# Two layers of conditioned attention on one core: the row maxima handed out to the steps by a length model, and two of the norms computed by GpSimd alone

## The chip, the cores and the metric

The kernel runs on 1 core of one Trainium2 chip. The metric is the device time of one execution in microseconds (us).

## The reference

x is (2, 1024, 256): two batches of 1024 tokens with 256 channels, all float32. Two layers follow each other, and both end in the same kind of tail.

```python
# layer 0: softmax attention with 16 heads of 16 channels
xn = layer_norm(x, norm_w, norm_b)
q, k = xn @ q_w + q_b, xn @ k_w + k_b                   # by head
att = softmax(einsum('bnhl,bmhl->bnmh', q, k) + (1 - mask) * -1e6, axis=2)
v = (xn @ v_w + v_b) * mask
y = einsum('bnmh,bmhl->bnhl', att, v)
scale, shift = split(silu(cond) @ emb_w + emb_b)
x = x + silu(layer_norm(y, sb_norm_w, sb_norm_b) * (1 + scale) + shift) @ out_w + out_b
# layer 1: linear attention with 8 heads of 32 channels
xn = layer_norm(x, ln_w, ln_b)
q = softmax(xn @ Wq + bq, axis=channels of a head)
k = softmax(xn @ Wk + bk + (1 - mask) * -1e6, axis=tokens)
v = (xn @ Wv + bv) * mask
y = q @ (k^T v)                                         # by head
x = x + silu(layer_norm(y, ln2_w, ln2_b) * (1 + scale1) + shift1) @ W_out + b_out
```

## The kernel before

Layer 0's attention is done in 128 steps (`STEPS`), numbered k. Eight steps (`NT`, one for each 128 keys) make one of 16 rows s (`SUBS`): one batch b, one half n of 512 queries, one group hg of four heads. TensorE computes the scores of a step, keys by queries, into four PSUM banks (sT, line 1072), ScalarE takes two exponentials (prob, line 895), and in the next step TensorE multiplies them with the values (line 1092). The softmax needs the maximum of each query beforehand. It comes from products of its own, the "maxima": a matmul of 128 queries by 512 keys into a bank (line 957) and a VectorE reduction of it (halfmax, line 1259). A row has 32 of them (`MAXES`), so there are 512, and they are made ahead of their row, 35 (`AHEAD`) before step 0. Behind the last of a row VectorE joins them (negmax, cpieces, lines 1262 to 1267), TensorE transposes the result (neg), and a DMA writes it into the query tile.

Everything else is laid into the steps: the projections of batch 1 (qk, v); for each half of batch 0 the norm of y (mid0), the output product (out0), the next layer's norm (in1), its keys, queries and values; then kT, qT, att, y1, the norm mid1, out1, and the start of the same for batch 1. `put` lays keys on half steps; small ones (`SMALL`: transposes and the like) may share a step, two large ones may not. From it come, for each step, what TensorE fills (`pe_at`) and what ScalarE (`act_at`) and VectorE (`dve_mid`, `dve_at`) do with it. A norm is laid by `layer_norm(kind, b, h, first)`: VectorE takes the statistics of four tiles at step `first` (line 1173) and joins them at `first + 1` (lines 1180 to 1183), GpSimd takes the power -0.5 and writes the normalised z (`normalise`, lines 667 to 683), and TensorE transposes z (T, line 985) at `first + 3`. Two norms, in0 of batch 1, are computed by GpSimd alone already (`alone`, lines 712 to 748): sums by halving, centring, squares, sums again, power, scaling.

In a step TensorE's order is: maxima of place 0, the scores, maxima of place 1, the values of the step before, maxima of place 2, maxima of place 3, the step's products. Those of place 3 are lent the banks of the scores. The others share a ring of three banks with the products. `places` gives a step with a large product the counts [1, 2, 0, 2] and others [2, 1, 0, 0] or [2, 0, 1, 0]; where a row's maxima would be late a step gets up to 5 or 6. VectorE goes through the same order. GpSimd's queue is one fixed list: set-up, the two norms of in0, bias rows, then norm after norm in the order of time, the mask row behind the first.

Of the kernel before, what the change touches and what calls it, by code (L numbers as in the profile page):

```python
# [21 lines left out]
def two_layer_conditioned_attention(  # L22
# [7 lines left out]
    ALU, ACT, AX = mybir.AluOpType, mybir.ActivationFunctionType, mybir.AxisListType  # L30

    B, T, D = x.shape
    P = 128
    NT = T // P
    KC = D // P
# [47 lines left out]
    with ctx:  # L83
# [144 lines left out]
        def put(keys, first):  # L228

            held = set(at.values())  # L230
            spot = 2 * first
            for key in keys:
                while spot in held or (key[0] not in SMALL and spot % 2 == 0):
                    spot += 1
                at[key] = spot
                spot += 1
            return (spot + 1) // 2

        layer_at = {}

        def layer_norm(kind, b, h, first):

            layer_at[kind, b, h] = first
            return put([("T", kind, b, h, kc) for kc in range(KC)], first + 3)

# [63 lines left out]
        for (kind, b, h), k in layer_at.items():  # L309
            for i in range(QT):  # L310
                (dve_mid if i < 2 else dve_at)[k].append(("stats", kind, b, h, i))
            dve_mid[k + 1].append(("aggr", kind, b, h))
            if kind[:3] == "mid":
                act_at[begins["T", kind, b, h, KC - 1]].append(("silu", kind, b, h))
                dve_at[begins["T", kind, b, h, KC - 1] + 1].append(("silu", kind, b, h))

        def places(k):
            kinds = [key[0] for key in pe_at[k]]
            if any(kind not in SMALL and kind not in ("y", "neg") for kind in kinds):
                return [1, 2, 0, 2]
            return [2, 0, 1, 0] if len(kinds) > 1 else [2, 1, 0, 0]


        LEAD = 2
        most_of = [6] * NT + [5] * (STEPS - NT)
        runs, taken_to = [], AHEAD  # L330
        for k in range(STEPS):
            s, c = divmod(k, NT)
            count = places(k) if k > 0 else [0, 2, 1, 2]
            most = min(len(stream), MAXES * (s + 2 + int(c >= 3))) - taken_to
            least = max(min(len(stream), MAXES * ((k + f + 1 + LEAD) // NT + 1)) - taken_to - sum(most_of[k + 1:k + f + 1]) for f in range(min(2 * NT, STEPS - k)))
            total = max(min(sum(count), most), min(least, most_of[k]))
            for place_of in (3, 2, 1, 0):
                while sum(count) > total and count[place_of] > 0:
                    count[place_of] -= 1
            for place_of, limit in ((0, 3), (2, 3), (1, 3)):  # L340
                while sum(count) < total and count[place_of] < limit:
                    count[place_of] += 1
            ends = [taken_to + sum(count[:i + 1]) for i in range(4)]
            runs.append([stream[first:end] for first, end in zip([taken_to] + ends[:3], ends)])
            taken_to = ends[3]
# [15 lines left out]

        ALONE = [("in0", 1, h) for h in range(NH)]
        LN = {key: i for i, key in enumerate(LNS + ALONE)}
        in_time = LNS[:NH] + ALONE + LNS[NH:]

        def layer_before(key):

            same = [other for other in in_time[:in_time.index(key)] if other[2] == key[2]]
            return same[-1] if same else None
# [261 lines left out]
        def _(pool):  # L631
# [79 lines left out]

            def alone(n, key):

                kind, b, h = key
                L, half = LN[key], slice(h * QT, (h + 1) * QT)
                steps = D.bit_length() - 1
                at_first = n * (2 * steps + 1)

                def sums(src, before):
# [7 lines left out]

                pool.wait_ge(x_in[4 + h], 16)
                sums(xs[:, b * NT + h * QT:b * NT + (h + 1) * QT, :], at_first)
                pool.wait_ge(halved, at_first + steps)  # L730
                pool.tensor_scalar(nmean[:, L, :], halves[:, :, 0], -1.0 / D, 0.0, op0=ALU.mult, op1=ALU.add).then_inc(alone_ready, 1)
                pool.wait_ge(alone_ready, 3 * n + 1)
                gone = unit[("T", *layer_before(key), KC - 1)]
                pool.wait_ge(gone.ready, gone.ready_at)
                for i in range(QT):
                    t = h * QT + i
                    pool.tensor_scalar(z[:, t, :], xs[:, b * NT + t, :], 1.0, nmean[:, L, i:i + 1], op0=ALU.mult, op1=ALU.add).then_inc(centred, 1)
                pool.wait_ge(centred, QT * (n + 1))
# [15 lines left out]
            pool.wait_ge(brow_ready, 2)  # L754
            for n, key in enumerate(ALONE):
                alone(n, key)
            pool.wait_ge(row_in, 16 * 2)
            add_bias("in0", 0, 0)
            add_bias("in0", 1, 0)
            for key in on_pool:  # L760
                normalise(key)
                if key == ("mid0", 0, 0):
                    mask_row(0)
                if key == ("in1", 0, 1):
                    add_bias("in1", 0, 1)
                if key == ("mid1", 0, 1):
                    mask_row(1)
# [653 lines left out]
```

## Time and profile before

| | us |
|---|---|
| median of 3 runs | 604.26 (602.32 to 608.66) |
| the profiled execution, its own time | 604.09 |
| its span in the profile | 602.3 |
| TensorE busy (PE) | 563.3 |
| VectorE busy (DVE) | 450.8 |
| ScalarE busy (ACT) | 337.3 |
| GpSimd busy (POOL) | 105.2 |

Busy times are sums over the span; a busy TensorE is not one at its peak, since its matmuls are pipelined. PEld is TensorE's weight load, which overlaps its matmuls.

### The profile page before, as it was taken

The numbers are of one execution on the slowest core, as the hardware profiler recorded it, in microseconds if no ns is written. First come the engines' busy times: TensorE is split into PE (matmuls) and PEld (weight loads), VectorE is DVE, ScalarE is ACT, GpSimd is POOL, SyncE is SP. The second block draws the span as 40 slices with busy tenths as digits, with TensorE's granted clock in tenths as the row PEclk, the third lists the DMA queues.
The fourth block names the chain that finished last, engine by engine and source line by source line (L and its number), as shares of the span: only waits on it lengthen the run. The fifth ranks groups of instructions, "written<-read, shape, count | busy, mean of one in ns | idle before, by whom it ended". The sixth has DMA issues, their size and how long they took to land. (4 is left out here: it accounts for less than half of the span.)

```text
span 602.3 us, 8434 instructions
## 1 busy us (share of the span) xinstructions
PE 563.3 (94%) x3068; PEld 272.1 (45%) x3068; DVE 450.8 (75%) x893; ACT 337.3 (56%) x410; POOL 105.2 (17%) x175
## 2 busy tenths in 40 slices
PE   7998899999998899999989999999989999989987
PEld 6453453334333343443334444554435543525775
DVE  6687677787788998888886989769979897305644
ACT  2522565555686756468637565664765565781431
POOL 4288000340000401000020140000432001002411
PEclk9998999999999999999966999999989999999999
DMA  4273981677301122104301010011102100000002
GB/s 131 91 153 63 218 249 45 158 181 169 90 2 28 32 52 54 29 1 83 78 5 28 2 28 0 1 28 36 27 1 64 35 3 1 1 1 0 2 2 70
DMA packets 18613, 33.74 MB, mean 56 GB/s; under 512 B 3963, under 2 KB 10483, under 8 KB 17805
## 3 DMA queue, kind: packets, MB, share of 16 engines
q1 hardware_dynamic: 18462, 33.18, 22.7%
q8 instruction: 25, 0.41, 0.3%
q14 instruction: 16, 0.12, 0.1%
q10 hardware_dynamic: 110, 0.03, 0.0%
HBM read 19.29 MB, written 13.52 MB: 54 GB/s over the span
## 5 line engine op out<-in xcount | busy, mean ns | idle before, releaser
L895 ACT ACTIVATE prob<-sT 128x1024 f32<-128x1024 f32 x256 | 247.7, 1023 | 129.2 <-PE sT L1072 129.0
L1259 DVE TENSOR_REDUCE halfmax<-bank 128x1 f32<-128x512 f32 x424 | 269.2, 684 | 59.2 <-PE bank L957 57.1
L957 PE MATMUL bank<-ks,qs 50*128 50x512 f32 x424 | 156.3, 487 | 17.4 <-DVE halfmax L1259 11.2
L1092 PE MATMUL bank<-prob,vp 128*17 128x512 f32 x1024 | 139.0, 615 | 0.6 <-ACT prob L895 0.6
L957 PEld LDWEIGHTS bank<-ks,qs 50*128 50x128 f32 x424 | 63.8, 189 | 132.0 <-DVE halfmax L1259 76.7
L1072 PE MATMUL sT<-qs,ks 52*128 52x512 f32 x512 | 106.7, 429 | 4.9 <-DVE halfmax L1259 1.9
L667 POOL TENSOR_TENSOR rstd<-var,neghalf 128x4 f32<-128x4 f32 x12 | 12.2, 1017 | 403.2 <-DVE var L1183 403.2
L1072 PEld LDWEIGHTS sT<-qs,ks 52*128 52x128 f32 x512 | 54.6, 191 | 22.3 <-ACT prob L895 11.0
L1259 DVE TENSOR_REDUCE halfmax<-sT 128x1 f32<-128x512 f32 x88 | 56.9, 685 | 7.6 <-PE sT L957 6.5
L932 PE MATMUL bank<-w,hT 128*128 128x256 f32 x152 | 38.7, 388 | 0.3 <-ACT hT L817 0.3
L1092 PEld LDWEIGHTS bank<-prob,vp 128*17 128x17 f32 x1024 | 17.1, 96 | 40.7 <-issue 37.2
L704 POOL TENSOR_TENSOR xs<-xs,bias_rows 128x256 f32<-128x256 f32 x32 | 23.4, 730 | 57.6 <-DMA bias_rows<-in_L_cond_b_out 54.9
L932 PEld LDWEIGHTS bank<-w,hT 128*128 128x128 f32 x152 | 26.5, 190 | 8.7 <-issue 4.5
L957 PEld LDWEIGHTS sT<-ks,qs 50*128 50x128 f32 x88 | 8.3, 183 | 36.6 <-ACT prob L895 36.6
L957 PE MATMUL sT<-ks,qs 50*128 50x512 f32 x88 | 22.2, 494 | 0.0
L1279 DVE RECIPROCAL rden<-bank 128x16 f32<-128x16 f32 x16 | 4.0, 252 | 20.4 <-PE bank L980 20.4
L992 PE MATMUL bank<-hT,wqk 128*128 128x512 f32 x36 | 17.7, 614 | 0.0
L824 ACT ACTIVATE late<-bank,cols 128x512 fp32r<-128x512 f32 x9 | 6.2, 687 | 20.4 <-PE bank L992 20.4
L817 ACT ACTIVATE hT<-bank,modB,modA 128x512 f32<-128x512 f32 x12 | 9.0, 779 | 14.7 <-PE bank L985 14.5
L985 PE MATMUL bank<-ident,z 128*128 128x128 f32 x96 | 14.8, 293 | 2.3 <-POOL z L695 1.7
L934 PE MATMUL bank<-brow,ones 128*128 128x256 f32 x36 | 16.8, 468 | 0.0
L1144 PE MATMUL bank<-wv,ident 128*128 128x512 f32 x34 | 15.8, 595 | 0.9 <-issue 0.9
(182 smaller groups left out, 558.4 us busy)
## 6 DMA issues: line engine op xcount, KB each, us to landing
stack_rows<-late SPq DMA_DIRECT2D x12, 512.0 KB, 6.6
qs<-stack_rows SPq DMA_DIRECT2D x30, 192.0 KB, 3.5
ks<-stack_rows SPq DMA_DIRECT2D x14, 384.0 KB
stack_rows<-late SPq DMA_DIRECT2D x17, 256.0 KB, 5.0
xs<-in_x SPq DMA_DIRECT2D x4, 256.0 KB, 3.7
xs<-in_x SPq DMA_DIRECT2D x2, 512.0 KB, 4.6
late<-in_L_cond_emb_w SPq DMA_DIRECT2D x1, 1024.0 KB, 8.3
late<-in_L_cond_W_emb SPq DMA_DIRECT2D x1, 1024.0 KB, 11.5
```

The source lines that it names most:

```text
L667: pool.tensor_tensor(rstd[:, L, :], var[:, L, :], neghalf[:, :], op=ALU.pow).then_inc(pow_ready, 1)
L704: pool.tensor_tensor(xs[:, t, :], xs[:, t, :], bias_rows[:, row, :], op=ALU.add).then_inc(biased, 1)
L895: act.activation(prob[:, c % 2, 2 * u:2 * u + 2, :].rearrange("p j n -> p (j n)"), sT[u][:, :], ACT.Exp).then_inc(exp_done, 1)
L932: last = pe.matmul(o[:, i * D:(i + 1) * D], hT[:, kc, tokens], w[:, kc, :], start=(kc == 0), stop=(kc == KC - 1 and row is None))
L934: last = pe.matmul(o[:, i * D:(i + 1) * D], ones[:, :], brow[:, row, :], start=False, stop=True)
L957: last = pe.matmul(o, qs[rows, s % SLOTS, c, t * P:(t + 1) * P], ks[rows, hg, c, half * HALF:(half + 1) * HALF], start=True, stop=True)
L985: last = pe.transpose(o[:, i * P:(i + 1) * P], z[:, h * QT + i, kc * P:(kc + 1) * P], ident[:, :])
L992: last = pe.matmul(o, wqk[:, kc, hg, :], hT[:, kc, n * HALF:(n + 1) * HALF], start=(kc == 0), stop=(kc == KC - 1))
L1072: last = pe.matmul(sT[u][:, two * HALF:(two + 1) * HALF], ks[rows, hg, u, c * P:(c + 1) * P], qs[rows, s % SLOTS, u, :], start=True, stop= ...
L1092: last = pe.matmul(acc[32 * j:32 * j + VW, :], vp[:, b, c, hg * GH + j, :], prob[:, c % 2, 2 * u + two, :], start=(c == 0), stop=(c == NT ...
L1144: pe.matmul(B8[7], ident[:, :], wv0[:, :, :].rearrange("p k d -> p (k d)"), start=True, stop=True)
L1259: dve.tensor_reduce(halfmax[:, s % 2, r, half:half + 1], o, axis=AX.X, op=ALU.max, negate=True).then_inc(u.done, 1)
```

## The change

1. The loop that gave each step its number of maxima is replaced. A model gives a step's length from what TensorE and VectorE have in it (`PE_WORK`, `DVE_WORK`; `length` is a sixth-power mean of both sums). Going through the steps, as long as the maxima handed out are fewer than are due two steps later, one more is given to that present or earlier step whose modelled length grows least; no step has more than 6, and none is given before its buffers allow it (`upper`). `places` turns the number into the four places.

2. The norms mid0 and in1 of batch 0's first half (`POOL_NORMS`) are taken from VectorE and computed by GpSimd with `alone`, which now takes its input and its scratch tile as arguments (the weights `wqk` are the scratch). Their transposes stand six steps behind the norm's `first` and not three, and what follows in that half moves with them.

```diff
--- before.py
+++ after.py
@@ -238,10 +238,12 @@
 
         layer_at = {}
 
+        POOL_NORMS = [("mid0", 0, 0), ("in1", 0, 0)]
+
         def layer_norm(kind, b, h, first):
 
             layer_at[kind, b, h] = first
-            return put([("T", kind, b, h, kc) for kc in range(KC)], first + 3)
+            return put([("T", kind, b, h, kc) for kc in range(KC)], first + (6 if (kind, b, h) in POOL_NORMS else 3))
 
         def layer_end(kind, b, h, first):
 
@@ -307,9 +309,10 @@
         dve_at[4].append(("cond",))
         dve_at[begins["values", 0, 3] + 2].append(("recips", 0))
         for (kind, b, h), k in layer_at.items():
-            for i in range(QT):
-                (dve_mid if i < 2 else dve_at)[k].append(("stats", kind, b, h, i))
-            dve_mid[k + 1].append(("aggr", kind, b, h))
+            if (kind, b, h) not in POOL_NORMS:
+                for i in range(QT):
+                    (dve_mid if i < 2 else dve_at)[k].append(("stats", kind, b, h, i))
+                dve_mid[k + 1].append(("aggr", kind, b, h))
             if kind[:3] == "mid":
                 act_at[begins["T", kind, b, h, KC - 1]].append(("silu", kind, b, h))
                 dve_at[begins["T", kind, b, h, KC - 1] + 1].append(("silu", kind, b, h))
@@ -317,29 +320,44 @@
 
 
 
+        PE_WORK = {"T": 0.5, "kT": 0.5, "qT": 0.5, "y": 0.45, "neg": 0.3, "vec2": 0.3, "embT": 0.5, "att": 1.0, "y1": 1.0}
+        DVE_WORK = {"stats": 0.38, "aggr": 0.75, "silu": 1.1, "y": 0.75, "neg": 0.3, "qk": 0.75, "out0": 0.7, "out1": 0.7, "keys": 0.75,
+                    "queries": 1.4, "qsum": 1.2, "recips": 0.7, "y1": 0.7, "att": 0.35, "vec2": 0.2, "embT": 0.5, "cond": 0.2}
+        LEAD = 2
+
+        def has_product(k):
+            return any(key[0] not in SMALL and key[0] not in ("y", "neg") for key in pe_at[k])
+
+        def length(k, count):
+            pe_work = 1.85 + sum(PE_WORK.get(key[0], 1.95) for key in pe_at[k]) + (0.24 if has_product(k) else 0.13) * count
+            dve_work = sum(DVE_WORK[key[0]] for key in dve_mid[k] + dve_at[k]) + 0.69 * count
+            dve_work += 0.6 * sum(key[0] == "keys" and key[2] == NH - 1 for key in dve_at[k])
+            return (pe_work ** 6 + dve_work ** 6) ** (1 / 6)
+
+        counts = [0] * STEPS
+        counts[0] = 5
+
+        def upper(k):
+            return min(len(stream), MAXES * (k // NT + 2 + int(k % NT >= 3))) - AHEAD
+
+        for k in range(STEPS):
+            while sum(counts[:k + 1]) < min(len(stream), MAXES * ((k + 1 + LEAD) // NT + 1)) - AHEAD:
+                free = [i for i in range(1, k + 1) if counts[i] < 6 and all(sum(counts[:j + 1]) < upper(j) for j in range(i, k + 1))]
+                best = min(free, key=lambda i: length(i, counts[i] + 1) - length(i, counts[i]))
+                counts[best] += 1
+
+
 
         def places(k):
-            kinds = [key[0] for key in pe_at[k]]
-            if any(kind not in SMALL and kind not in ("y", "neg") for kind in kinds):
-                return [1, 2, 0, 2]
-            return [2, 0, 1, 0] if len(kinds) > 1 else [2, 1, 0, 0]
-
-
-        LEAD = 2
-        most_of = [6] * NT + [5] * (STEPS - NT)
+            if k == 0:
+                return [0, 2, 1, 2]
+            if has_product(k):
+                return ([0, 0, 0, 0], [1, 0, 0, 0], [1, 1, 0, 0], [1, 2, 0, 0], [1, 1, 0, 2], [1, 2, 0, 2], [2, 2, 0, 2])[counts[k]]
+            return ([0, 0, 0, 0], [1, 0, 0, 0], [2, 0, 0, 0], [2, 1, 0, 0] if len(pe_at[k]) < 2 else [2, 0, 1, 0], [2, 1, 1, 0], [3, 1, 1, 0], [3, 1, 2, 0])[counts[k]]
+
         runs, taken_to = [], AHEAD
         for k in range(STEPS):
-            s, c = divmod(k, NT)
-            count = places(k) if k > 0 else [0, 2, 1, 2]
-            most = min(len(stream), MAXES * (s + 2 + int(c >= 3))) - taken_to
-            least = max(min(len(stream), MAXES * ((k + f + 1 + LEAD) // NT + 1)) - taken_to - sum(most_of[k + 1:k + f + 1]) for f in range(min(2 * NT, STEPS - k)))
-            total = max(min(sum(count), most), min(least, most_of[k]))
-            for place_of in (3, 2, 1, 0):
-                while sum(count) > total and count[place_of] > 0:
-                    count[place_of] -= 1
-            for place_of, limit in ((0, 3), (2, 3), (1, 3)):
-                while sum(count) < total and count[place_of] < limit:
-                    count[place_of] += 1
+            count = places(k)
             ends = [taken_to + sum(count[:i + 1]) for i in range(4)]
             runs.append([stream[first:end] for first, end in zip([taken_to] + ends[:3], ends)])
             taken_to = ends[3]
@@ -359,9 +377,9 @@
         silus = [key[1:] for k in range(STEPS + 2) for key in act_at[k] if key[0] == "silu"]
         LNS += [("mid0", B - 1, 1), ("in1", B - 1, 1), ("mid1", B - 1, 0), ("mid1", B - 1, 1)]
 
-        ALONE = [("in0", 1, h) for h in range(NH)]
+        ALONE = [("in0", 1, h) for h in range(NH)] + POOL_NORMS
         LN = {key: i for i, key in enumerate(LNS + ALONE)}
-        in_time = LNS[:NH] + ALONE + LNS[NH:]
+        in_time = LNS[:NH] + ALONE[:NH] + sorted(layer_at, key=lambda key: layer_at[key]) + [key for key in LNS[NH:] if key not in layer_at]
 
         def layer_before(key):
 
@@ -709,12 +727,13 @@
                     there = mrow[:, n * HALF:(n + 1) * HALF]
                     pool.tensor_scalar(there, there, 1.0, BIG, op0=ALU.subtract, op1=ALU.mult).then_inc(mrow_ready, 1)
 
-            def alone(n, key):
+            def alone(n, key, halves):
 
                 kind, b, h = key
                 L, half = LN[key], slice(h * QT, (h + 1) * QT)
                 steps = D.bit_length() - 1
                 at_first = n * (2 * steps + 1)
+                tiles_in = y_all[:, b, half, :] if kind == "mid0" else xs[:, b * NT + h * QT:b * NT + (h + 1) * QT, :]
 
                 def sums(src, before):
                     width = D // 2
@@ -725,16 +744,23 @@
                         pool.tensor_tensor(halves[:, :, 0:width], there[:, :, 0:width], there[:, :, width:2 * width], op=ALU.add).then_inc(halved, 1)
                         width //= 2
 
-                pool.wait_ge(x_in[4 + h], 16)
-                sums(xs[:, b * NT + h * QT:b * NT + (h + 1) * QT, :], at_first)
+                if kind == "in0":
+                    pool.wait_ge(x_in[4 + h], 16)
+                else:
+                    last = unit[("y", (b * NH + h) * HG + HG - 1) if kind == "mid0" else ("out0", b, 2 * h + 1)]
+                    pool.wait_ge(last.done, last.done_at)
+                sums(tiles_in, at_first)
                 pool.wait_ge(halved, at_first + steps)
                 pool.tensor_scalar(nmean[:, L, :], halves[:, :, 0], -1.0 / D, 0.0, op0=ALU.mult, op1=ALU.add).then_inc(alone_ready, 1)
                 pool.wait_ge(alone_ready, 3 * n + 1)
-                gone = unit[("T", *layer_before(key), KC - 1)]
+                former = layer_before(key)
+                gone = unit[("T", *former, KC - 1)]
                 pool.wait_ge(gone.ready, gone.ready_at)
+                if former in silus:
+                    pool.wait_ge(silu_ready[former], 1)
                 for i in range(QT):
                     t = h * QT + i
-                    pool.tensor_scalar(z[:, t, :], xs[:, b * NT + t, :], 1.0, nmean[:, L, i:i + 1], op0=ALU.mult, op1=ALU.add).then_inc(centred, 1)
+                    pool.tensor_scalar(z[:, t, :], tiles_in[:, i, :], 1.0, nmean[:, L, i:i + 1], op0=ALU.mult, op1=ALU.add).then_inc(centred, 1)
                 pool.wait_ge(centred, QT * (n + 1))
                 pool.tensor_tensor(halves[:, :, :], z[:, half, :], z[:, half, :], op=ALU.mult).then_inc(halved, 1)
                 sums(halves, at_first + steps + 1)
@@ -752,13 +778,17 @@
             pool.wait_ge(wrep_ready, 1 + 4 * KC)
             pool.tensor_tensor(brow[32:33, :, :], braw[32:33, :, :], bhi[32:33, :, :], op=ALU.subtract).then_inc(brow_ready, 1)
             pool.wait_ge(brow_ready, 2)
-            for n, key in enumerate(ALONE):
-                alone(n, key)
+            for n in range(NH):
+                alone(n, ALONE[n], halves)
+            by_four = wqk.rearrange("p k g m -> p (k g m)").rearrange("p (t d) -> p t d", t=QT)
             pool.wait_ge(row_in, 16 * 2)
             add_bias("in0", 0, 0)
             add_bias("in0", 1, 0)
-            for key in on_pool:
-                normalise(key)
+            for key in in_time[2 * NH:2 * NH + len(layer_at)]:
+                if key in POOL_NORMS:
+                    alone(ALONE.index(key), key, by_four)
+                else:
+                    normalise(key)
                 if key == ("mid0", 0, 0):
                     mask_row(0)
                 if key == ("in1", 0, 1):
```

## Rows read from the trace of the kernel before

**Rows 1.** The page's slices: TensorE clock granted, in tenths, 40 slices of the span.

```profile
PEclk9998999999999999999966999999989999999999
```

**Rows 2.** Windows by stage: start:end, length, busy us of each engine, clock, DMA.

```profile
59.64:537.10 477.46, 454.66 (x2589) 204.24 (x2585) 378.03 (x715) 297.29 (x346) 54.03 (x78) 0.97 0.23 55
0.00:59.64 59.64, 52.92 (x203) 29.59 (x205) 42.74 (x101) 19.34 (x33) 35.65 (x82) 0.97 0.45 109
537.10:602.30 65.20, 55.77 (x280) 38.30 (x280) 30.00 (x78) 20.71 (x31) 15.48 (x16) 1.00 0.05 17
```

**Rows 3.** Groups by line and shape, whole span: busy us, mean ns, idle before.

```profile
L1259 DVE TENSOR_REDUCE halfmax<-bank 128x1 f32<-128x512 f32 x424 | 269.2, 684 | 59.2 <-PE bank L957 57.1
...
L957 PE MATMUL bank<-ks,qs 50*128 50x512 f32 x424 | 156.3, 487 | 17.4 <-DVE halfmax L1259 11.2 <-DVE late L1330 2.4 <-DVE y_all L1282 1.0
...
L1173 DVE BATCH_NORM_STATS2 stats<-xs 128x6 f32<-128x256 f32 x24 | 8.5, 411 | 0.1
```

**Rows 4.** Sum rows of windows: steps by class, product, small, y1, plain.

```profile
sum 200.60, PE 193.05 PEld 91.45 DVE 164.12 ACT 101.17 POOL 13.64; mean PE 4.83 PEld 2.29 DVE 4.10 ACT 2.53 POOL 0.34
...
sum 71.13, PE 70.06 PEld 35.59 DVE 48.87 ACT 57.99 POOL 11.26; mean PE 3.89 PEld 1.98 DVE 2.71 ACT 3.22 POOL 0.63
...
sum 17.13, PE 15.93 PEld 8.14 DVE 16.48 ACT 7.76 POOL 3.38; mean PE 3.98 PEld 2.03 DVE 4.12 ACT 1.94 POOL 0.84
...
sum 162.52, PE 150.53 PEld 57.46 DVE 143.33 ACT 110.24 POOL 25.75; mean PE 2.69 PEld 1.03 DVE 2.56 ACT 1.97 POOL 0.46
```

**Rows 5.** Windows: steps 20-32, 34-39, 66-71; then steps 4, 77, 60.

```profile
154.37:185.87 31.50, 30.53 (x203) 10.83 (x202) 26.36 (x47) 25.96 (x30) 0.00 (x0) 1.00 0.11 29
189.45:209.84 20.39, 17.68 (x108) 7.17 (x107) 19.06 (x41) 14.02 (x16) 7.23 (x8) 1.00 0.04 12
301.82:328.90 27.08, 25.34 (x107) 9.90 (x107) 19.32 (x41) 14.13 (x15) 3.37 (x6) 0.62 0.03 9
78.69:83.52 4.83, 4.83 (x30) 2.73 (x28) 3.40 (x7) 2.66 (x4) 0.00 (x0) 1.00 1.02 199
...
347.95:351.79 3.84, 3.64 (x26) 1.77 (x24) 3.06 (x8) 3.47 (x5) 3.45 (x6) 1.00 0.00 0
284.01:287.61 3.60, 3.21 (x20) 1.39 (x18) 3.40 (x7) 1.94 (x3) 0.00 (x0) 1.00 0.02 5
```

**Rows 6.** Windows: before the clock's fall and in it; step 101.

```profile
302.60:306.06 3.46, 2.43 (x17) 1.02 (x9) 3.46 (x9) 1.76 (x3) 0.00 (x0) 1.00 0.00 0
306.06:326.54 20.48, 19.77 (x74) 7.82 (x75) 12.71 (x28) 9.65 (x11) 3.37 (x6) 0.50 0.00 1
...
444.80:449.70 4.90, 4.14 (x18) 1.49 (x17) 3.41 (x7) 1.94 (x2) 0.00 (x0) 0.65 0.00 0
```

**Rows 7.** Timeline of GpSimd: first and last part of norm in0 (1, 0).

```profile
28.40 1.27 POOL L725 TENSOR_TENSOR late<-xs 128x512 f32<-128x512 f32 x1
...
42.64 1.84 POOL L748 TENSOR_SCALAR z<-z,rstd 128x256 f32<-128x256 f32 x4
```

**Rows 8.** Timeline: y; exponential and transposes of step 37; out0.

```profile
188.20 0.42 DVE L1282 TENSOR_TENSOR y_all<-bank,rden 128x256 f32<-128x256 f32 x1
...
200.57 1.94 ACT L895 ACTIVATE prob<-sT 128x1024 f32<-128x1024 f32 x2 [1.33 <-PE sT L1072]
...
202.12 0.66 PE L985 MATMUL bank<-ident,z 128*128 128x128 f32 x4
...
218.64 0.69 DVE L1314 TENSOR_TENSOR xs<-xs,bank 128x512 f32<-128x512 f32 x1 [0.41 <-PE bank L932]
219.32 1.02 ACT L895 ACTIVATE prob<-sT 128x1024 f32<-128x1024 f32 x1 [3.07 <-PE sT L1072]
```

**Rows 9.** Timeline at 51 us; the source line of cpieces (ns, min/median/max).

```profile
51.00 1.89 POOL L739 TENSOR_TENSOR late<-z 128x1024 f32<-128x1024 f32 x1
51.01 1.91 DVE L1267 TENSOR_TENSOR cpieces<-negmax,cpieces 128x16 fp32r<-128x16 f32 x1
...
L1267 DVE TENSOR_TENSOR cpieces<-negmax,cpieces x16: 174/176/1909, 51.0 to 510.4; 128x16 fp32r<-128x16 f32 x16
```

## The prediction

> **What bounds the kernel now.** I read the clock line of the page first, then the three stages, then the steps inside the middle stage. The kernel is 128 steps of score matmuls, two exponentials and value matmuls; between these lie 477 of the 512 "maxima" (one TensorE matmul and one VectorE reduction each), the projections' products, transposes and norms. The steps take 477.5 of 602.3 us; TensorE is busy in 454.7 of them, VectorE in 378.0 [rows 2]. The order on each engine is fixed, so a step lasts as long as the engine that has more in it, and what the change can win is the time in which one engine is full and the other waits. On VectorE a maximum is a reduction of 684 ns; the 487 ns of its matmul are mostly latency, which overlaps in a stream [rows 3].
>
> I cut the trace at the first exponential of each step (256 rows of that line, two a step) and put each step into a class by what TensorE has besides scores, values and maxima. Four sums result [rows 4]. The 40 steps with a large product: 200.6 us, TensorE busy 193.1, VectorE 164.1, so TensorE sets them. The 18 with transposes or another small product: 71.1 us, TensorE 70.1. The 4 steps of y1: 17.1, VectorE 16.5 and TensorE 15.9. The 56 "plain" ones, with nothing or only y or neg: 162.5 us, TensorE 150.5, VectorE 143.3; neither is full on the whole, because two kinds are mixed. Thirteen plain steps with 3 maxima (154.37 to 185.87) take 31.50/13 = 2.42 us each, TensorE at 97%; one with 5 takes 3.60, and there VectorE is busy 3.40 and TensorE, waiting for banks, 3.21 [rows 5]. Steps 34 to 39, with the statistics of norm mid0 (0, 0) and four steps of 5 maxima, take 20.39 us with TensorE busy 17.68. That is what a different hand-out can recover.
>
> There is a second loss. The clock line falls in two slices [rows 1]: TensorE ran at half clock (1.2 instead of 2.4 GHz) from 306.06 to 326.54 us; just before, VectorE had been busy all the time and TensorE 2.43 of 3.46 us [rows 6]. Steps 66 to 71 repeat steps 34 to 39 operation for operation and took 27.08 instead of 20.39 us [rows 5]: the fall cost 6.7. In a short second one step 101, with 5 maxima, took 4.90 instead of 3.60 [rows 5, 6], 1.3 more. Together 8.0. All four executions at hand are above 602 us, so I take such falls as usual in this kernel.
>
> **Part 1, the hand-out.** I worked both loops through from the code's numbers. Product steps: 202 maxima before, 216 after (22 steps have 6, 13 have 5, five have fewer). Transposes and the like: 63 in 18 steps before, 76 in 17 after (ten have 5). y1: 20 before, 13 after. Plain: 192 in 56 steps before (twelve have 5), 172 in 57 after: 22 steps with 4, 22 with 3, 12 with 1 or 2, one with none; those of the last two kinds mostly hold statistics or silu. Nothing else is added on TensorE, so I price each class.
>
> Product steps, on TensorE: 14 more matmuls. The low end is 0: a product step with 6 maxima took 4.83 us, no longer than the mean of the class, 200.6/40 = 5.02, nearly all with 5. The high end is the busy time that two more matmuls add in a plain step, (3.21 - 30.53/13)/2 = 0.43 us [rows 4, 5]. I take half of that, 0.22, since a full stream hides the latency part: +3.1 us (0 to +6.0). The reductions are covered: VectorE has 36 us to spare in the class and gets 14 x 0.684 = 9.6.
>
> Plain and transposes together took 162.5 + 71.1 = 233.6, and 225.6 without the 8.0 of half clock, nearly all of which lies in them. After: 22 plain steps with 3 maxima at 2.42 are 53.3. The 22 with 4 have no row. The low end is TensorE's, 2.42 + 0.22 = 2.64; the high end adds a whole reduction, 2.42 + 0.684 = 3.10; VectorE's own work is 26.36/13 + 0.684 = 2.71 [rows 5], and I take 2.9, since two nearly full engines lose some to each other: 63.8. The 12 with 1 or 2 maxima hold at most four statistics of 0.41 [rows 3] or as much: 0.684 + 1.64 = 2.3, put at 2.4, together 28.8; the one with none 2.6. Ten steps with 5 maxima and two transposes at 3.84 [rows 5] are 38.4; the seven other small ones at 4.1, a little above the class mean of 3.95 since y and att fall to them, 28.7. Sum 215.6, a gain of 10.0; the ends of the 4-maxima price make it 5.6 to 15.7.
>
> y1: VectorE's 16.5 loses 7 x 0.684 and has 11.7, TensorE's 15.9 loses 7 x 0.22 and has 14.4; with some gaps 15.0, a gain of 2.1 (1 to 3).
>
> **Part 2, two norms on GpSimd.** For mid0 (0, 0) and in1 (0, 0) VectorE loses four statistics, the aggregation and two small operations each, about 2.4 us; this is in the classes above. GpSimd gains for each what it does for in0 (1, 0): 28.40 to 44.48, 16.1 us [rows 7]. It is idle otherwise in both stretches; behind the first norm stands the mask row, not needed before step 52, behind the second nothing before step 66. The scratch is a weight tile last read in step 17.
>
> The transposes wait for z on TensorE's queue, and behind them stand all later scores and maxima, so a late z stops everything. Mid0: the last y is written at 188.62 [rows 8], z would be there at 204.8. Steps 34 to 39 now have 3, 3, 3, 3, 4, 3 maxima and no statistics: 5 x 2.42 + 2.9 = 15.0. In the step that had these transposes they began 1.55 us after its first exponential (202.12 against 200.57) [rows 8]. Step 34 began at 189.45 and can begin 0.6 earlier, as one maximum fewer stands before its scores. So the transposes of step 40 are reached at 188.85 + 15.0 + 1.55 = 205.4, 0.6 us behind z. In1: the last addition of out0 ended at 219.33, when the next step's first exponential began (219.32) [rows 8]; z comes 16.2 us later, the transposes after steps 45 to 50 (3, 4, 3, 3, 3, 3 maxima, 15.0) and 1.55, 0.4 us behind z. Both just fit; I put 0.5 us of waiting for each, +1.0 (0 to +3, the latter if plain steps are as short as 2.25 and the norm takes 0.5 more).
>
> GpSimd beside VectorE is not free. cpieces, a small VectorE operation with two inputs in SBUF and a median of 176 ns, took 1909 when it began at 51.01, beside a GpSimd product from 51.00 to 52.89 [rows 9]: they ended together. Mid0's norm now lies over step 35, where a set of maxima ends and cpieces is made. GpSimd's operations there are halvings of at most 1.27 us [rows 7], so at most 1.1 us on VectorE, once, which a step of 3 maxima (VectorE busy 2.03 of 2.42) partly absorbs: 0.2, inside the +1.0. In1's norm meets no end of a set.
>
> The Trainium skill (GPSIMD Engine Reference, section 8, Key points) has the rule: the two engines share SBUF interfaces and contend when the VectorE instruction has two SBUF inputs. The row agrees. By the rule held against every such operation the sum would be 1.1 us worse, by how the rows absorb it 0.2.
>
> The products behind the two norms move by three steps (out0 from 40 and 41 to 43 and 44) and up to six (values from 51 and 52 to 57 and 58), into plain steps; from step 69 on all stand where they stood. The last stage, 65.2 us [rows 2], is untouched.
>
> **Sum.** +3.1 - 10.0 - 2.1 + 1.0 = -8.0 us at an equal clock. The clock fell after a stretch in which VectorE was full, with 5 maxima beside statistics, and TensorE waited. After the change statistics stand beside 1 maximum (3 in step 96, as before), and 5 stand only beside transposes or products, so I take the 8.0 us as gone. Against the profiled execution of 604.1 us (span 602.3 and 1.8 around it; the median, 604.3, is practically the same): 604.1 - 8.0 - 8.0 = 588; since a short fall may remain, 589.
>
> **Rivals.** A, as above: 589 us, chance 0.48. B, the clock falls as long as before, since TensorE waits elsewhere (VectorE is fuller in 22 steps with 4 maxima than it was with 3): 604.1 - 8.0 = 596, chance 0.32. For it: none of four executions shows a run without falls. Against it: with TensorE at 97% from 154 to 186 us it did not fall. C, the hand-out is worth little: a fourth maximum costs 0.68 and a product's sixth 0.43, so -8.0 + 4.4 + 2.9 = -0.7, 603.4 us with the falls as before and 595 without; 0.15. D, slower: z is late. If the norm takes GpSimd 20 us instead of 16.1 (each of its 28 operations held up 0.14 us by VectorE), TensorE stands still for 3.3 us ahead of the transposes in steps 40 and 51, and if the clock falls behind each at 6.7 us: 604.1 - 16.0 + 2 x (3.3 + 6.7) = 608. It decides from a norm of about 18 us on; 0.05.
>
> The Trainium skill (TensorE: Matmul & The Clock Gate, Part 1) ties the clock to how busy TensorE has been, which allows both B and D; the row shows a fall with TensorE 70% busy, not idle.
>
> **Range.** The unknown prices spread A over 583 to 594 and B over 591 to 601. 8 in 10: 584 to 601. Under 1% (598 to 610) a measurement of this kernel can't tell a change from none. Faster by over 1%: nearly all of A, three quarters of B, a half of C, 0.78; within 1%, 0.17; slower, 0.05.
>
> **What would show it.** Steps 20 to 32 at some 2.8 us in the mean instead of 2.42, steps 34 to 39 at 15 instead of 20.4, product steps with 6 maxima at 4.9 to 5.3; two GpSimd stretches of 16 us, the first from about 193; TensorE waiting for GpSimd's z under 1 us; no half clock after step 0. It is wrong if steps with 4 maxima reach 3.1, if the wait for z is over 2 us, or if half clock appears elsewhere.

## The result and the profile after

The changed kernel takes 595.11 us in the median of four executions (593.50 to 597.03), against 606.46 for four of the kernel before in the same comparison (602.32 to 614.23); the ratio is 0.9865 with a 95% interval of 0.9825 to 0.9904. So it is 1.35% faster, where 2.5% was forecast (589 us). The time is inside the range of 584 to 601, but the size of the gain is about half of the forecast. (Ratios leave out executions that lie 1.5% above the fastest of their kernel, as 614.23 does; the fit further down takes all.)

The page of the profiled execution (595.13 us, span 593.3), the lines that answer to [rows 1] and the busy shares:

```profile
span 593.3 us, 8459 instructions
PE 562.8 (95%) x3068; PEld 274.0 (46%) x3068; DVE 447.4 (75%) x873; ACT 337.5 (57%) x410; POOL 127.3 (21%) x219
...
PEclk9999999999999999999999998999999999999999
```

The half clock of slices 21 and 22 is gone. Windows: the sum rows of the same classes of steps (product, small, plain), as in [rows 4]:

```profile
sum 205.70, PE 198.28 PEld 93.69 DVE 169.26 ACT 101.10 POOL 15.90; mean PE 4.96 PEld 2.34 DVE 4.23 ACT 2.53 POOL 0.40
...
sum 72.71, PE 72.47 PEld 36.51 DVE 55.17 ACT 56.43 POOL 11.85; mean PE 4.26 PEld 2.15 DVE 3.25 ACT 3.32 POOL 0.70
...
sum 149.82, PE 142.67 PEld 54.51 DVE 133.17 ACT 112.04 POOL 46.54; mean PE 2.50 PEld 0.96 DVE 2.34 ACT 1.97 POOL 0.82
```

Windows: steps 20 to 32, 34 to 39, 66 to 71, the whole middle stage, as in [rows 2, 5]:

```profile
152.97:188.91 35.94, 34.95 (x214) 13.51 (x212) 32.27 (x57) 26.10 (x29) 0.00 (x0) 1.00 0.09 24
191.87:207.06 15.19, 14.93 (x95) 5.31 (x94) 13.51 (x26) 11.63 (x13) 13.32 (x26) 1.00 0.06 16
303.15:320.23 17.08, 16.23 (x100) 6.33 (x100) 14.62 (x34) 13.86 (x16) 3.40 (x6) 1.00 0.06 18
59.28:528.11 468.83, 453.04 (x2589) 203.70 (x2585) 374.57 (x695) 297.45 (x347) 77.67 (x125) 1.00 0.23 57
```

The stretches that were forecast one by one came as forecast: steps 20 to 32 take 2.76 us each (2.8), steps 34 to 39 15.19 (15.0). The middle stage is 8.6 us shorter, which is about what the half clock alone had cost (8.0). What the small steps had to give is not there: 17 of them take 72.7 us, where 67.1 were in the sum.

The GpSimd norms, timeline of GpSimd and of the first transposes behind them (compare [rows 7, 8]):

```profile
191.99 1.28 POOL L744 TENSOR_TENSOR wqk<-y_all 128x512 f32<-128x512 f32 x1 [65.12 <-DVE y_all L1312]
...
206.27 1.84 POOL L774 TENSOR_SCALAR z<-z,rstd 128x256 f32<-128x256 f32 x4
...
208.83 0.42 PEld L1015 LDWEIGHTS bank<-ident,z 128*128 128x128 f32 x4 [0.25 <-DVE halfmax L1289]
...
240.99 1.84 POOL L774 TENSOR_SCALAR z<-z,rstd 128x256 f32<-128x256 f32 x4
...
244.57 0.66 PE L1015 MATMUL bank<-ident,z 128*128 128x128 f32 x4
```

Mid0's norm lasts 16.12 us and its z is complete at 208.11, 0.72 us before TensorE's transposes (forecast 0.6); in1's is 1.7 us early (0.4). No time is lost there.

### The profile page after: what moved, and what is told of

Same layout as the page of the kernel before. It is cut to its first block and busy times, and to the rows that moved or that the text cites. A ratio compares the mean times of both kernels' runs of the same rounds, so it can differ in the third digit from the quotient of the medians.

```text
span 593.3 us, 8459 instructions
## 1 busy us (share of the span) xinstructions
PE 562.8 (95%) x3068; PEld 274.0 (46%) x3068; DVE 447.4 (75%) x873; ACT 337.5 (57%) x410; POOL 127.3 (21%) x219
## 5 line engine op out<-in xcount | busy, mean ns | idle before, releaser
L1122 PE MATMUL bank<-prob,vp 128*17 128x512 f32 x1024 | 135.5, 601 | 0.7 <-ACT prob L925 0.6
L987 PEld LDWEIGHTS bank<-ks,qs 50*128 50x128 f32 x428 | 62.9, 183 | 128.2 <-DVE halfmax L1289 81.6
L1102 PE MATMUL sT<-qs,ks 52*128 52x512 f32 x512 | 104.6, 422 | 6.2 <-ACT prob L925 4.1
L685 POOL TENSOR_TENSOR rstd<-var,neghalf 128x4 f32<-128x4 f32 x10 | 10.2, 1016 | 290.8 <-DVE var L1213 290.8
L1102 PEld LDWEIGHTS sT<-qs,ks 52*128 52x128 f32 x512 | 52.1, 185 | 25.7 <-ACT prob L925 15.9
L1289 DVE TENSOR_REDUCE halfmax<-sT 128x1 f32<-128x512 f32 x84 | 54.3, 686 | 8.3 <-PE sT L987 7.7
L1344 DVE TENSOR_TENSOR xs<-xs,bank 128x512 f32<-128x512 f32 x12 | 8.3, 688 | 10.9 <-PE bank L962 10.9
```

Source lines behind the costliest of these rows:

```text
L685: pool.tensor_tensor(rstd[:, L, :], var[:, L, :], neghalf[:, :], op=ALU.pow).then_inc(pow_ready, 1)
L987: last = pe.matmul(o, qs[rows, s % SLOTS, c, t * P:(t + 1) * P], ks[rows, hg, c, half * HALF:(half + 1) * HALF], start=True, stop=True)
L1102: last = pe.matmul(sT[u][:, two * HALF:(two + 1) * HALF], ks[rows, hg, u, c * P:(c + 1) * P], qs[rows, s % SLOTS, u, :], start=True, stop= ...
L1122: last = pe.matmul(acc[32 * j:32 * j + VW, :], vp[:, b, c, hg * GH + j, :], prob[:, c % 2, 2 * u + two, :], start=(c == 0), stop=(c == NT ...
L1289: dve.tensor_reduce(halfmax[:, s % 2, r, half:half + 1], o, axis=AX.X, op=ALU.max, negate=True).then_inc(u.done, 1)
```

## How the clock and the rest were separated

Each execution comes with its span and mean granted clock. Of the kernel before there are 27 beside the first four. They run from 595.15 to 608.79 us, and the clock explains most of it: two at 1.000 have spans of 593.3 and 593.8 us, one at 0.977 has 605.3, one at 0.966 has 606.9. I call span x (1 - mean clock) the lost clock and fitted, over 85 executions in 14 series (the changed kernel ran in two), span = a constant for each program + slope x lost clock. The slope is 0.65 (standard error 0.04), the residual 1.4 us, so a constant from four executions is good to about 0.7. (A lost clock of 10 us is 20 us at half clock.)

| kernel | executions | mean lost clock, us | span at full clock, us |
|---|---|---|---|
| before | 27 | 10.4 | 593.4 |
| changed (both series) | 8 | 2.4 | 591.7 |
| e1 hand-out alone | 4 | 3.9 | 595.1 |
| e2 norms alone | 4 | 11.9 | 594.7 |
| e3 places 3, 0, 2, 0 | 4 | 2.4 | 591.6 |
| e4 before, matmuls repeated | 4 | 1.8 | 594.2 |
| e5 before, half reads | 4 | 0.0 | 570.0 |
| e6 changed, half reads | 4 | 0.0 | 572.6 |
| e7 four behind | 4 | 8.5 | 598.5 |
| e8 four norms | 10 | 3.2 | 592.8 |
| e9 ScalarE in the model | 4 | 3.1 | 588.7 |
| e10 and product price | 4 | 4.2 | 589.9 |
| e11 silu steps refilled | 4 | 3.6 | 592.4 |

The gain of the change, 7.0 us in the mean of all these executions (602.1 to 595.1), is 0.65 x (10.4 - 2.4) = 5.2 us of clock and 1.7 us at equal clock (standard error 0.7).

This fit takes the three chips of the experiments as equal, and they are not quite. At full clock the kernel before has 593.4 us on the chip of e1 to e4, 592.7 on that of e5 to e8 and 594.9 on that of e9 to e12 (standard errors 0.4 to 0.5). With an offset for each chip in the fit, the changed kernel is 2.8 us below the kernel before (0.9) and e9 another 3.3 below it, while e1 stays 1.8 above the kernel before, e2 1.3 and e8 0.1. So the gain at equal clock is 1.7 to 2.8 us, and a difference of two rows of the table that ran on different chips is uncertain by some 2 us.

## The experiments

All are compared with the kernel before on the same chip. The first four shared one chip and seven executions of it (median 602.44).

**e1, the hand-out alone.** Edit on the changed kernel:

```diff
-        POOL_NORMS = [("mid0", 0, 0), ("in1", 0, 0)]
+        POOL_NORMS = []
```

> The new hand-out alone; both norms stay on VectorE with their transposes three steps behind. If the gain is the clock's (theory 1: the falls come from plain steps in which VectorE is full and TensorE waits, and the hand-out takes these away), half clock covers under 10 us of the steps and the time is 594 to 599. If the gain came from the norms' move (theory 2), the time is 601 to 606 and half clock stays at 20 us or more.

Measured: 599.77 us (597.64 to 600.59), 0.9992 (0.993 to 1.0055). The lost clock falls to 3.9 us, which is 8 us at half clock, as theory 1 has it; the profiled execution has one fall, ahead of step 0. But at full clock the kernel is 1.7 us slower than before, so it ends no faster than the kernel before with its falls, and just outside the 594 to 599 of theory 1.

**e2, the norms alone.** The loop and `places` of the kernel before, put back into the changed one.

> The two norms on GpSimd and their transposes six steps behind, with the old hand-out, whose plain steps with 5 maxima number thirteen instead of twelve. Theory 1 (the hand-out removes the clock falls): half clock stays, 15 us or more of the steps, time 601 to 605. Theory 2 (the norms' move does it): 595 to 599. GpSimd's z is in time in either, since the steps behind the norms are no shorter than with the new hand-out.

Measured: 603.46 us (600.50 to 610.02), 1.0043 (0.9962 to 1.0123); lost clock 11.9 us. Theory 1: the hand-out removes the falls, the norms' move does not. At full clock 594.7, no gain either. The falls of its profiled execution lie at other places than before: 17 us ahead of and in steps 0 and 1, and 6.8 us from step 42 on, a plain one with 5 maxima, none in steps 66 to 71.

**e3, other places.** In `places` of the changed kernel:

```diff
+            if counts[k] == 5 and len(pe_at[k]) >= 2 and not has_product(k):
+                return [3, 0, 2, 0]
```

> The changed kernel, but steps with transposes and 5 maxima give them to the places as 3, 0, 2, 0, as the kernel before did, and not 3, 1, 1, 0. Theory: the same work of step 77 took 3.84 us before and 4.46 after the change because the maximum of place 1 holds the values up until VectorE frees a bank; then ten such steps win 0.3 to 0.6 us each and the time is 590 to 592. Rival: the boundary of the step only moves, the next step pays it back, and the time is that of the changed kernel, 594 to 596.

Measured: 595.46 us (592.66 to 596.49), 0.9918 (0.9854 to 0.9983), the changed kernel's time. The ten steps together became 1.1 us shorter than in e12 (41.8 and 42.9), and the ten steps behind them 1.7 us longer (34.5 and 32.7): the boundary of a step moved. Step 77 itself, at 4.48, did not move at all. My theory fell, and with it the reading of one step's length as its price.

**e4, the kernel before with more for TensorE.**

```diff
+                    if key in again:
+                        pe.matmul(o, qs[rows, s % SLOTS, c, t * P:(t + 1) * P], ks[rows, hg, c, half * HALF:(half + 1) * HALF], start=True, stop=True)
                     last = pe.matmul(o, ...)
```

`again` holds the maxima of place 0 of the twelve plain steps with 5.

> The kernel before, in which the matmuls of the three maxima of place 0 are issued twice in the twelve plain steps with 5 maxima (36 matmuls more, the same result written twice). They add about 0.7 us of TensorE work to steps in which it waits for VectorE. Theory 1 (the clock falls because TensorE has too little to do there): no half clock between 60 and 540 us and 595 to 598 us, faster than the kernel before although nothing is taken away. Rival (the falls have another cause): half clock as before and 604 to 612 us.

Measured: 596.50 us (595.88 to 599.79), 0.9954 (0.9888 to 1.002). Windows of its profile, steps 34 to 39 and 66 to 71:

```profile
188.71:209.00 20.29, 18.19 (x113) 7.87 (x112) 18.85 (x41) 14.03 (x15) 7.25 (x8) 1.00 0.04 13
301.59:321.89 20.30, 18.17 (x113) 7.84 (x112) 18.85 (x41) 14.03 (x15) 3.38 (x6) 1.00 0.05 14
```

The twins are now equal; in [rows 5] they were 20.39 and 27.08. Work that does nothing takes the lost clock from 10.4 to 1.8 us: the falls in the steps come from TensorE's waiting beside a full VectorE. This is not said of every fall: the kernel before, e1 and e12 have one of 3.4 us ahead of step 0, and e3, e8 and e10 have one of 3.4 us in step 57, a product step. The run also gives the classes of the kernel before at full clock: product 200.6, small and plain 156.98 + 69.36 = 226.3 us, the whole stage 470.1. Its sum rows, plain and small:

```profile
sum 156.98, PE 147.44 PEld 58.99 DVE 142.45 ACT 110.15 POOL 25.85; mean PE 2.63 PEld 1.05 DVE 2.54 ACT 1.97 POOL 0.46
...
sum 69.36, PE 68.28 PEld 34.80 DVE 49.33 ACT 58.06 POOL 11.20; mean PE 3.79 PEld 1.93 DVE 2.74 ACT 3.23 POOL 0.62
```

**e5 and e6, both kernels with half of each reduction.**

```diff
-  dve.tensor_reduce(halfmax[...], o, axis=AX.X, op=ALU.max, negate=True)
+  dve.tensor_reduce(halfmax[...], o[:, 0:HALF // 2], axis=AX.X, op=ALU.max, negate=True)
```

> The kernel before, whose 512 reductions read only the first 256 of a bank's 512 columns (so the maxima are of half the keys): VectorE's part of a maximum falls from 0.68 to about 0.42 us, 120 us less in all, and TensorE has all its work. This shows how much of the time is TensorE's waiting for banks. Theory (at full clock the kernel before loses little to VectorE, since TensorE is idle for only 22 us of the steps): 575 to 585 us. Rival (imbalance costs much): below 570.

> The changed kernel with the same half reads. If both kernels have the same TensorE limit, this one comes to within 3 us of the kernel before with half reads, and what both lose to VectorE is read from the two differences: theory, 12 to 18 us in either, so that the hand-out moved the waits for banks and did not remove them. Rival: the changed kernel loses clearly less to VectorE (under 8 us) than the kernel before.

Measured: 571.64 us (571.29 to 572.49), 0.9572 (0.954 to 0.9605), and 574.96 (572.78 to 575.28), 0.9618 (0.9579 to 0.9657), beside 599.54 of the kernel before; the clock is 1.000 in all eight executions. Groups of the two traces, the reduction and the wait of TensorE's weight loads for it (76.7 and 81.6 us with whole reductions):

```profile
L1259 DVE TENSOR_REDUCE halfmax<-bank 128x1 f32<-128x256 f32 x424 | 162.6, 420 | 110.5 <-PE bank L957 104.9
...
L957 PEld LDWEIGHTS bank<-ks,qs 50*128 50x128 f32 x424 | 60.0, 183 | 113.6 <-DVE halfmax L1259 57.1 <-issue 29.1 <-DVE late L1330 4.2
```

```profile
L1289 DVE TENSOR_REDUCE halfmax<-bank 128x1 f32<-128x256 f32 x428 | 164.4, 420 | 115.0 <-PE bank L987 109.8
...
L987 PEld LDWEIGHTS bank<-ks,qs 50*128 50x128 f32 x428 | 59.9, 183 | 113.1 <-DVE halfmax L1289 59.7 <-issue 28.9 <-DVE late L1360 4.2
```

With reductions shorter by 264 ns the order is reversed: the changed kernel is the slower by 2.6 us (standard error 1.0, same chip). At full clock the shorter reductions are worth 23.4 us to the kernel before (593.4 - 570.0) and 19.1 to the changed one, more than either expectation had for them: 571.64 lies below the 575 to 585 of the theory, and above the rival's 570, and the 12 to 18 us of the second theory were exceeded in both. The waits for banks are shorter and not gone, so VectorE's whole price may be larger. The change as a whole removed about 4 us of VectorE's holding up, half of what I had forecast, and made the rest 3 us longer; the first figure compares chips and is uncertain by about 2 us. What in the rest is longer was not isolated; e9 and e11 bear on it.

**e7, the transposes four steps behind.** `first + (4 if ...` instead of 6.

> The changed kernel with the transposes of the two GpSimd norms four steps behind and not six. After the change they began 0.7 us behind z; two steps earlier, 5 to 6 us for mid0 and 5 for in1, TensorE must stand still for z: 4 to 5.5 us each. Theory: a wait there costs its length and the time is 602 to 607, with a clock fall possible behind each wait. Rival: the other engines catch up meanwhile and it costs less than half, 596 to 600.

Measured: 606.28 us (604.27 to 606.89), 1.0139 (1.009 to 1.0187). Its timeline at step 38 (the idle time of each engine and its releaser in brackets):

```profile
208.01 0.71 PEld L1015 LDWEIGHTS bank<-ident,z 128*128 128x128 f32 x4 [5.71 <-issue]
208.04 1.09 PE L1015 MATMUL bank<-ident,z 128*128 128x128 f32 x4 [5.42 <-POOL z L774]
```

and two windows of it, from step 37 on; the third value from the right of each row is the granted clock, ahead of the two DMA columns:

```profile
199.00:206.00 7.00, 3.62 (x24) 0.91 (x16) 3.70 (x6) 3.37 (x4) 6.13 (x11) 1.00 0.00 0
206.00:212.80 6.80, 4.76 (x20) 2.32 (x20) 2.26 (x4) 2.60 (x3) 5.71 (x6) 0.50 0.06 11
```

The two waits that TensorE gets, 5.4 and 4.0 us, are 9.4 us long and cost 6.8 at full clock (8.6 with an offset for each chip). The clock fell in the course of each of them, at 206.0 and 247.0 us, for 6.8 us, which costs another 4.0 in the mean for both. This is rival D of the prediction in its mechanism; its total of 608 is near for another reason, since it had shorter waits (3.3 us each) and dearer falls (6.7 us each, where the two cost 2.0 each here). The six steps of the change avoid it by 0.7 us.

**e8, four norms on GpSimd.** `POOL_NORMS` also holds ("mid0", 0, 1) and ("in1", 0, 1).

> The changed kernel with the norms mid0 and in1 of batch 0's second half on GpSimd too, their transposes six steps behind; what follows moves by three to six steps and still ends in time. VectorE loses another 4.8 us, in steps that hold 1 or 2 maxima now. Theory (TensorE and its waits for banks set the time): 593 to 597, no gain that can be measured. Rival (VectorE's work sets it): 588 to 592.

Measured: 597.13 us (592.86 to 598.95, ten executions), 0.9958 (0.9919 to 0.9996). At full clock 592.8, against 591.7 of the changed kernel and 592.7 of the kernel before on the same chip: the move gained nothing, and the rival fell. The products that moved with the two norms changed as well, so what less work on VectorE is worth by itself is not shown.

**e9 and e10, ScalarE in the model; e11, the silu steps refilled; e12, the changed kernel beside them.** The last chip (before: 602.61).

```diff
+        ACT_WORK = {"T": 0.75, "silu": 1.06, "qk": 0.69, "v": 0.84, "values": 0.84, "emb": 0.6, "kT": 0.6, "qT": 0.6, "kexp": 1.15, "qexp": 0.63, "cond": 0.2}
...
-            return (pe_work ** 6 + dve_work ** 6) ** (1 / 6)
+            act_work = 1.85 + sum(ACT_WORK[key[0]] for key in act_at[k]) + 0.6 * (k > 0 and k % NT == 0)
+            return (pe_work ** 6 + dve_work ** 6 + act_work ** 6) ** (1 / 6)
```

e10 has 0.34 for 0.24 in `pe_work` as well; e11 has only "silu": 0.0 for 1.1 in `DVE_WORK`.

> The changed kernel with a third sum in the length model: ScalarE's, 1.85 us for the two exponentials and what else it has in the step (0.75 for each transposed tile, 1.06 for the tanh of a silu, 0.69 for qk and so on). Ten steps with transposes then get 6 maxima instead of 5, and product steps 208 instead of 216. Theory (ScalarE bounds the steps with transposes, so that maxima there are free): 588 to 593 us. Rival (in those steps TensorE waits for banks as well, so a sixth maximum costs as much as anywhere): 594 to 599.

> As the one before, and a further maximum in a product step is priced at 0.34 us of TensorE in the model instead of 0.24. Product steps then hold 192 maxima and plain ones 182. If a sixth maximum in a product step costs about 0.45 us in truth, as nine of the steps that have one more than before show, this is another 2 us faster than the kernel with ScalarE's sum alone; rival: the plain steps with 4 cost as much, and the two are the same within 2 us.

> The changed kernel with the silu at 0 instead of 1.1 us in the model's VectorE sum: steps 41, 70, 97 and 100, which lasted 1.81 us, the length of their two exponentials, with 1, 2, 0 and 2 maxima, get 3, 4, 2 and 3; step 107 gets 6 instead of 3, and nine others one less. Theory (these steps and the ones ahead of them are bound by ScalarE, so the change took maxima out of places where they were free): 2 to 4 us faster than the changed kernel run beside it. Rival (VectorE needs the room for the silu): the same or up to 3 us slower.

> The changed kernel itself, as the measure for the three beside it on the same chip: 593 to 597 us.

The reason for them, windows of the changed kernel: steps 40 and 41, steps 96 and 97, and step 66 alone.

```profile
207.06:213.78 6.72, 6.25 (x41) 2.66 (x39) 4.34 (x8) 6.65 (x9) 4.91 (x5) 1.00 0.85 150
420.02:426.59 6.57, 5.80 (x39) 2.39 (x37) 5.27 (x16) 6.54 (x9) 2.59 (x4) 1.00 0.08 16
...
303.15:305.03 1.88, 1.84 (x13) 0.43 (x12) 1.88 (x7) 1.88 (x2) 0.00 (x0) 1.00 0.10 20
```

and of the kernel before the first two's counterparts, steps 37 and 38, 96 and 97:

```profile
200.57:207.24 6.67, 6.23 (x40) 2.55 (x38) 5.61 (x12) 6.26 (x7) 2.88 (x2) 1.00 0.00 0
427.23:433.83 6.60, 6.46 (x42) 2.92 (x40) 6.14 (x19) 6.57 (x9) 0.91 (x1) 1.00 0.02 3
```

In the changed kernel ScalarE is busy for 6.65 of 6.72 us in the first pair. It held 8 maxima before and holds 6 now, and lasts the same; the second pair held 6 and holds 3.

Measured: e9 591.88 us (590.20 to 596.22), 0.9814 (0.9744 to 0.9884); e10 594.72 (591.22 to 596.94), 0.9862 (0.9788 to 0.9936); e11 596.48 (595.83 to 597.48), 0.988 (0.9824 to 0.9936); e12 595.27 (592.47 to 597.04), 0.9855 (0.9791 to 0.9918). e9 is the fastest version: 588.7 us at full clock, 3.3 below e12 on the same chip (standard error about 0.9), a time as its theory has it. The higher price of e10 adds nothing.

Where e9's gain lies is read from the sum rows of e12 and e9 (product, small and plain of each):

```profile
sum 204.12, PE 196.69 PEld 93.16 DVE 169.16 ACT 101.11 POOL 13.24; mean PE 4.92 PEld 2.33 DVE 4.23 ACT 2.53 POOL 0.33
sum 72.74, PE 72.51 PEld 36.52 DVE 55.13 ACT 56.43 POOL 11.86; mean PE 4.27 PEld 2.15 DVE 3.24 ACT 3.32 POOL 0.70
sum 149.94, PE 142.66 PEld 54.45 DVE 133.24 ACT 112.01 POOL 47.59; mean PE 2.50 PEld 0.96 DVE 2.34 ACT 1.97 POOL 0.83
...
sum 199.63, PE 193.92 PEld 91.98 DVE 163.84 ACT 101.04 POOL 16.46; mean PE 4.85 PEld 2.30 DVE 4.10 ACT 2.53 POOL 0.41
sum 76.26, PE 72.47 PEld 34.74 DVE 61.30 ACT 57.34 POOL 13.12; mean PE 4.26 PEld 2.04 DVE 3.61 ACT 3.37 POOL 0.77
sum 146.35, PE 139.38 PEld 54.25 DVE 131.07 ACT 111.94 POOL 46.26; mean PE 2.45 PEld 0.95 DVE 2.30 ACT 1.96 POOL 0.81
```

The product steps give 4.5 us back for 8 maxima fewer and the plain ones 3.6 for 5 fewer; the small ones take 3.5 more for 13 more, and y1 takes 1.3 more. So maxima in the small steps were cheap and not free. The ten that now hold 6 (nine had 5, step 96 had 3) take 46.1 us for 43.6: eight of them 0.1 us more each, steps 69 and 96 1.2 and 0.6.

e11 is no faster than e12 (592.4 and 592.0 at full clock). Steps 41, 97 and 100 took their 2, 2 and 1 more maxima at 0.03 us or less. Step 70 took 0.7 us more and step 107 0.3, and the steps ahead of these two another 0.5 and 0.9. Ten steps have one fewer (the expectation says nine); they gave 2.3 us back, 1.8 of it in steps 68 and 117. So ScalarE's bound is real in three steps, but that the maxima taken from the silu steps are what the change lost is not shown.

## Why the prediction was wrong in size

**What bounds the kernel**: right in the mechanism. e5 shows 23 us of VectorE's holding up at full clock, more than I expected.

**The hand-out, product steps**, +3.1: measured 204.1 (e12, no fall inside) against 200.6, +3.5. Right.

**The hand-out, plain and transposes**, "Sum 215.6, a gain of 10.0": this is the step that failed. The baseline was right (225.6; e4 has 226.3). After the change the two classes take 149.8 + 72.7 = 222.5 us, a gain of 3.8. I had priced kinds of steps by single favourable rows instead of by their class: 3 maxima in a plain step at 2.42 from steps 20 to 32, where all 44 of them had a mean of 2.62 and the 22 after the change have 2.58 (+3.5 us); 5 maxima with transposes at 3.84 from step 77, where the four of before had 4.35 at full clock (e4: two at 3.84 and two, with a silu's tanh on ScalarE, at 4.86) and the ten after have 4.29 (+4.5); 4 maxima came at 2.98 for 2.9 (+1.8); the seven other small steps, of which one holds 5 as well, at 4.3 (+1.1). Against that, steps with 0 to 2 came at 2.1 instead of 2.4 (-4). A step is measured from exponential to exponential, so a step whose neighbours pay for it looks cheap, as the ten steps of e3 and the ten behind them show.

**y1**, -2.1: measured 14.5 against 17.1, -2.6. **GpSimd's norms**, +1.0: nothing was lost, 16.1 us and 0.72 us of slack as worked out; cpieces in step 35 took 0.17 us while GpSimd halved beside it, so the contention that [rows 9] and the Trainium skill (GPSIMD Engine Reference, section 8, Key points) allow did not strike there; in the set-up, beside the longer product, it did again, with 1.90 us.

These give +3.5 - 3.8 - 2.6 = -2.9; the whole stage has -2.7 between e4 (470.1 us) and e12 (467.4), on another chip, and the fit -1.7, or -2.8 with an offset for each chip. Forecast: -8.0.

**The clock**, "I take the 8.0 us as gone": the cause is right (e4, e5, e7), the size was off twice. The four executions above 602 us were taken for the rule, but the loss varies from none to 0.037 of the span, and its mean, 10.4 us of lost clock, costs 6.8. And a part stays: 2.4, or 1.6 us. In the profiled execution it fell in step 83, for 3.4 us, after a stretch in which TensorE waited twice for a bank, with VectorE not full. Half clock elsewhere was one of the prediction's signs of being wrong:

```profile
363.71:367.12 3.41, 2.56 (x16) 1.23 (x18) 2.73 (x5) 2.12 (x3) 0.00 (x0) 1.00 0.00 0
367.12:370.53 3.41, 3.41 (x13) 1.23 (x6) 2.09 (x5) 0.33 (x1) 0.00 (x0) 0.50 0.00 0
```

So -5.2 for -8.0. Of the rivals, C (the hand-out is worth little) came nearest, together with A's clock: "595 without" the falls was its figure. That figure was met by luck in good part. C put the loss into a fourth maximum at 0.68 us and a product step's further one at 0.43; measured are 0.40 (2.98 - 2.58) and 0.25 (3.5/14). The loss lay in the prices of 3 maxima in a plain step and of the steps with transposes, which C took over from A.

**What stays open**: why the changed kernel is 2.6 us slower with the shorter reductions, and why the two halves of the change lose 1 to 2 us alone and win 1.7 to 2.8 together at full clock. The losses alone are about two standard errors each, the other two differences about three. What starts the short falls in product steps was not tried either.

## What to carry to other kernels

Price a kind of step by the mean of all its instances and check the price on the sum of the stage, never by the stretch that shows it best: a step that borrows from its neighbours looks cheap. A balance over two engines should name the third: pairs of steps that already lasted as long as ScalarE's work won nothing when maxima were taken out of them, and some of them took more for next to nothing. Before explaining a few microseconds, fit the time over the granted clock of many executions, with the kernels compared on the same chip; here two thirds to three quarters of the gain were the clock.

## What was unexpected of the hardware

The same program on the same chip ran at mean clocks from 0.963 to 1.000, and its time followed at 0.65 us for each us of lost clock; 36 repeated matmuls, which do nothing for the result, removed most of it. At equal clock the same program still differed by 2.2 us between two chips (594.9 and 592.7). A reduction of 256 columns instead of 512 took 420 ns instead of 684; if the time grows evenly between, 156 ns of it do not scale with the columns (an estimate from these two).
